# Four copies of the experts' sums in place of six, in a kernel of two transformer layers on one core

## The reference

```
idx, wts = router(x)                      # 6 of 64 experts for each token
every expert takes the first CAP = 64 of its tokens, of all 2048
h  = relu(xd @ w1[e].T) ** 2              # 64 experts, 256 -> 128
yd = h @ w2[e].T                          # 128 -> 256
y[token] += yd[e, slot] * gate            # six experts add to one token
out = x + shared_expert(x) + y
```

## Time and profile before

| | |
|---|---|
| median of 3 runs | 1400.0 us (1399.84 to 1404.95) |
| span of the profiled execution | 1398.3 us |
| busy share: TensorE, DVE, ACT, POOL | 83%, 65%, 47%, 42% |
| first to last start of an add | 1291.81 to 1352.80 us |
| loading, summing and storing the copies | 1356.6 to 1398.3 us |
| moved by DMA in this last stretch | 14.70 MB |

### The profile page before, as it was taken

The page is one execution under the profiler, slowest core; times in us unless marked ns, Lnnn a source line. Parts: engine busy times, 40 slices in busy tenths (PEclk is TensorE's granted clock), DMA queues, the critical chain, the costliest instruction groups (busy, mean ns, idle before and its releaser), DMA issues.

```text
span 1398.3 us, 24417 instructions
## 1 busy us (share of the span) xinstructions
PE 1163.0 (83%) x8422; PEld 748.5 (54%) x8422; DVE 908.5 (65%) x1814; ACT 655.5 (47%) x1544; POOL 586.1 (42%) x789
## 2 busy tenths in 40 slices
PE   3799988798899977998899977989999886979940
PEld 2355556565565555664555655655555664644520
DVE  4488875555878766556888765656888755571417
ACT  3655523565455523657444334656545234620630
POOL 1255561220387742210677822210777711225760
PEclk9899999799999999899999997989999998989975
DMA  7366633700243314501333236101433529166879
GB/s 306 115 191 188 199 106 87 91 3 19 85 136 114 109 56 80 61 3 33 117 121 111 97 87 72 21 20 42 125 120 121 176 72 133 36 223 232 158 130 365
DMA packets 107499, 159.56 MB, mean 114 GB/s; under 512 B 11633, under 2 KB 68593, under 8 KB 106737
## 3 DMA queue, kind: packets, MB, share of 16 engines
q1 hardware_dynamic: 92592, 129.64, 35.4%
q0 software_dynamic: 9216, 19.98, 5.5%
q10 hardware_dynamic: 5568, 8.39, 1.7%
HBM read 104.55 MB, written 40.83 MB: 104 GB/s over the span
## 4 chain that ended last, share of the span: by engine, by line
PE 48%; DVE 19%; POOL 11%; issue 9%; ACT 8%; DMA 3%; ACTq 1%; SPq 0%; POOLq 0%; DVEq 0%
PE bank L1067 12%; DVE pool_c L1537 5%; PE bank L1109 4%; PE bank L992 4%; PE bank L1225 3%; POOL joint L1998 3%; PE bank L1249 3%; DVE joint L1553 3%; PE bank L1264 2%; POOL xn L2005 2%; PE bank L1088 2%; PE bank L1103 2%; PE bank L1337 2%; PE bank L1207 2%; PE bank L1096 2%
## 5 line engine op out<-in xcount | busy, mean ns | idle before, releaser
L1067 PE MATMUL bank<-xnT,joint 128*128 128x512 f32 x544 | 274.6, 629 | 20.8 <-DVE pool_c L1537 15.6
L1998 POOL TENSOR_TENSOR joint<-joint 128x512 f32<-128x512 f32 x128 | 168.6, 1318 | 244.7 <-DVE joint L1553 244.1
L1537 DVE SCALAR_TENSOR_TENSOR pool_c<-bank,params,pool_c 128x511 f32<-128x511 f32 (+2 forms) x216 | 161.3, 747 | 85.9 <-ACT pool_c L716 80.4
L1067 PEld LDWEIGHTS bank<-xnT,joint 128*128 128x128 f32 x544 | 100.3, 198 | 125.2 <-issue 93.8
L1708 DVE TENSOR_REDUCE nmax<-bank 128x1 f32<-128x512 f32 (+3 forms) x176 | 109.9, 639 | 74.6 <-PE bank L1226 73.4
L755 ACT ACTIVATE joint<-bank,dt_ 128x64 f32<-128x64 f32 x512 | 112.1, 343 | 27.8 <-PE bank L992 27.7
L1109 PE MATMUL bank<-wout,pool_c 128*128 128x256 f32 x512 | 123.4, 384 | 1.2 <-DVE pool_c L1578 1.2
L1109 PEld LDWEIGHTS bank<-wout,pool_c 128*128 128x128 f32 x512 | 97.3, 193 | 35.3 <-issue 23.3
L1992 POOL DMA_INDIRECT xslot<-xrow,slots x96 | 97.2, 1013 | 34.9 <-issue 20.3
L857 ACT ACTIVATE pool_c<-bank 128x512 f32<-128x512 f32 (+1 forms) x176 | 91.4, 549 | 37.0 <-PE bank L1251 35.4
L725 ACT ACTIVATE pool_c<-pool_c 128x512 f32<-128x512 f32 x64 | 40.3, 629 | 135.9 <-DVE pool_c L1537 135.9
(11 more groups left out here) (266 smaller groups left out, 2419.1 us busy)
## 6 DMA issues: line engine op xcount, KB each, us to landing
pool_b<-dA_rows SPq DMA_DIRECT2D x64, 256.0 KB
pool_b<-dec_rows SPq DMA_DIRECT2D x96, 128.0 KB, 3.7
joint<-pool_b SPq DMA_DIRECT2D x96, 128.0 KB, 8.6
acc<-xrow SPq DMA_DIRECT2D x13, 640.0 KB, 6.5
joint<-dA_rows SPq DMA_DIRECT2D x32, 256.0 KB, 3.3
dA_late<-dA_rows SPq DMA_DIRECT2D x32, 256.0 KB, 4.1
xslot<-xrow SPq DMA_DIRECT2D x16, 321.0 KB, 4.7
pool_b<-xslot SPq DMA_DIRECT2D x64, 80.2 KB
```

Of the source, the lines that this page charges most:

```text
L1067: last = mm(bank[:, :], win[:, k, col:col + P], xnT[:, k, :], start=(k == 0), stop=(k == KD - 1))
L1537: ins = v.scalar_tensor_tensor(out=cv[:, n:L], in0=bank[:, 0:L - n], scalar=convw[:, ci, TAPS - 1 - n:TAPS - n], in1=cv[:, n:L], op0=ALU.m ...
L1998: M_ready.inc(p.tensor_tensor(M[u % 2][:, hs_, :], Lx[:, hs_, :], cbm[:, c * P:(c + 1) * P].unsqueeze(1).to_broadcast([P, 4, P]), ALU.mult))
```

## The change

`SETS` goes from 3 to 2, and the sum of a block loses one add:

```diff
-SETS = 3
+SETS = 2
 SUMS = 2 * SETS
...
                 dve.wait_ge(pair_sum.sem, pair_sum.last())
-                pair_sum.inc(v.tensor_tensor(parts_[0], parts_[0], parts_[2], ALU.add))
-                dve.wait_ge(pair_sum.sem, pair_sum.last())
-                final_sum.inc(v.tensor_tensor(parts_[0], parts_[0], parts_[4], ALU.add))
+                final_sum.inc(v.tensor_tensor(parts_[0], parts_[0], parts_[2], ALU.add))
```

## The result

With four copies the kernel takes 1405.0 us in the median (1402.5 to 1407.8) beside 1400.9 before: a ratio of 1.0029, 95% interval 1.0018 to 1.0040. The forecast was 1405.5. The 4.1 us of the medians are less than the 7 us that the prediction called about the least that can be told from no change, but the interval excludes 1.

The account below looks back on a forecast made before the run. POOL's adds were taken to bound the expert loop and DMA the summing. Loop +17.0, summing -11.3 and row 0 -0.2 gave +5.5 us on the 1400.0 median: 1405.5, with an 8-in-10 range of 1394 to 1414.

Parts of the forecast that it names:

- The bytes: Summing after the loop: 48 loads of 256 KB become 32, 4.19 MB less at some 389 GB/s, 10.8 us less.
- The lower bound of 10.6 us: Summing after the loop: least shortening expected, from bytes alone at the rate's upper end; 11.3 us was forecast.
- The wait that comes nearer: Expert loop: add i waits for add i-2, not i-3, so POOL waits on landings; 78.0 against 61.0, 17.0 us more.
- The step of (landing + 0.85) / 2: Expert loop: time per add when POOL, found idle, starts 0.85 us after its wait passes; 2.55 us early, 2.375 late.
- The 1.3 us carried over for adds 3 and 17: Expert loop: idle time before two adds that began late after their waits had passed, added to 76.7 us of steps.
- Row 0 and the prologue: Row 0's scans and prologue: 4.3 MB less zeroing saves 0.2 us, at most 0.8; other prologue changes nothing.
- Landings stay hidden: Rival, expert loop: adds land within 3.73 - 0.5 us, loop stays at 61 us, total 1388.5; chance 0.10.
- Crowded landings: Rival, expert loop: landings don't shorten as adds thin out and odd delays come through; +13.5, 1413.5 us; chance 0.20.

## Why the prediction was right, point by point

*The bytes.* Expected 10.8 us less to the last landing, measured 10.3; the rate was the trace's. Behind it 0.5 expected, 0.7 measured. Together 11.3 and 11.1. The lower bound of 10.6 us wasn't what its words say: at the upper end of the rate, 409 GB/s, 4.19 MB take 10.3. The run that read four copies alone has the summing at 30.4 us.

*The wait that comes nearer.* 17.0 expected, 16.3 measured. The step of (landing + 0.85) / 2 rested on two starts of the trace before, adds 8 and 23; it became the rule: 0.83 to 0.86 us at 25 of 30 adds. One of the 29 passes read as landings isn't one (add 7 had landed 0.7 us before POOL came to its wait), which is 0.03 us of the mean of 4.47. Landings were taken as 4.25 while tokens load and 3.9 after; they were 4.14 and 3.80. The 1.3 us carried over for adds 3 and 17 were the wrong size and half the wrong adds: add 3 was on time, and adds 9 and 17 each cost 1.18 us more than the others, 2.4 in all. The errors, -1.9 us by the landings and +1.1 by the late adds, cancel in part: with 4.14 and 3.80 the steps alone are 17 x 2.49 + 14 x 2.32 = 74.8, and 2.4 make it 77.2. The run with the nearer wait alone has 15.5 us of it with six copies.

*Row 0 and the prologue.* 0.2 us expected; the larger zeroing cost 0.5 (-0.7 to 2.0), and the scans of row 0 differ by 0.1. No more can be said.

*The rivals.* Landings stay hidden: fell, no add in any run landed sooner than 3.5 us after its start. The rule of the Trainium skill on which it could rest ("DMA: Bandwidth & Descriptors", Anatomy of one DMA — SWDGE), an estimate of 2.3 us for 128 KB, isn't borne out: with no other add and no token load beside it an add takes 3.8 us from the start of its issue. Crowded landings: it had two things right in part. The late adds 9 and 17 come into the open when POOL has no slack, and token loads do lengthen a landing, by 0.2 us. But early landings did shorten, from 4.47 to 4.14, and the mean over all adds is 4.04, under the 4.2 from which the rival was to decide. The forecast's own reason, that fewer adds under way leave the DMA engines less full, is no more than half borne out: from two adds to one nothing shortens.

*What was luck.* Not the mechanism, but the closeness. The medians moved by 4.1 us and the profile by 6.7, of which 1.4 arose in the first loads. A sum of differences good to 1 us was compared with medians that stray by 2 us, so that 1405.0 beside 1405.5 says no more than that the sum is right to a few us. Stage by stage, +16.3 and -11.1 against +17.0 and -11.3 are the better test.

## What to carry to other kernels

A buffer count that looks like memory traffic at one end may be the depth of a pipeline at the other: before taking a set away, compare the time from an operation's start to its landing with the steps that are left. What then waits costs the landing and the engine's start from idle as well (here 0.84 us, not 0.30). And if one half of a change gains while the other loses, make each alone, and read its stage in the profile beside the time: here they were worth -11.8 and +15.3 us from the first add on (-9.9 and +17.8 in the times), and a version that keeps the depth early and frees the set late is 1.4 us faster than before, by an interval that just excludes no change.

## What the runs showed of the hardware

POOL found idle starts an indirect DMA 0.83 to 0.86 us after the wait passes, against 0.30 us behind the instruction before it when that is still running; in kernels with three distances of the wait. At adds 9 and 17 it is 2.0 us, in all of them (not at add 25). What it is was not tried; in the traces of before and after no packet of the instruction queues lies between the wait's pass and the start of either, so it is not a load of code that moves just then.

An add alone takes 3.8 us from the start of its issue to the wait's pass, 1.56 of it the issue, and a second add beside it adds nothing to that.

The early adds of the run without token loads landed after 4.11 us where an instruction packet moved beside them and after 3.82 where none did.
